# A graph layer on one core: three PSUM banks in turn for the row sums, and exponentials written to SBUF in place

## The chip, the core and the metric

The kernel runs on one core of a Trainium2 chip. The core has four compute engines that work side by side, each through its own list of instructions in order: TensorE (PE, matrix products into PSUM), VectorE (DVE), ScalarE (ACT) and GpSimd (POOL). SyncE (SP) issues DMA transfers. They meet through semaphores. PSUM has eight banks of 128 partitions by 512 f32. The metric is the device time of one execution in microseconds (us), lower is better. A difference of about 0.3% is what the measurement can tell from no change.

## What is computed

One layer of a graph network on 6250 nodes with 128 features and 100000 edges sorted by destination:

```python
a_k = exp(relu(concat(h[src], h[dst]) @ W_att_k + b_att_k))     # k = 1, 2, 3, one number per edge
att_k = segment_sum(a_k, dst)
avg_a = (a_1 / att_1[dst] + a_2 / att_2[dst] + a_3 / att_3[dst]) / 3
m = avg_a * relu(relu(relu(h[src] @ W1 + b1) @ W2 + b2) @ W3 + b3)
h_neigh = segment_sum(m, dst) / maximum(degree, 1)
out = relu(concat(h, h_neigh) @ Wc1 + bc1) @ Wc2 + bc2
return layernorm(x + out)
```

## The kernel before

The message of an edge depends on its source node alone, so the kernel first makes a table in HBM with a row of 128 message features and 3 logits for each node (up to about 56 us). Then it works through the edges in groups of 256 (two tiles of 128 edges). The first 94 groups, whose destinations are the 384 nodes with the most edges, are not gathered. For them VectorE and TensorE count how many edges run between each source and each of these nodes (the counting stage, one-hot products of L1428 added to `counts` by L1711). The dense stage then multiplies these counts by the exponentials of all 49 blocks of 128 source nodes against the 384 nodes.

The other 297 groups are cut into 126 units, `first_order`. Unit 0 has two groups, units 1 to 23 have four, the rest two (the last one). For each tile of a unit GpSimd issues one gather, an indirect DMA that fetches 128 rows of the table into a ring of 12 places (`gath`, L1226). In nine early units (3, 5, ... 19) the second pair of groups is not gathered, because its messages are computed directly, so the gathers are 558. Unit n has to be summed before its places in the ring are used again.

All engines walk the same loop over steps i = 0 ... 125. What matters in a step, in each engine's own order:

- TensorE: `add_edges(i)` (L1405 sums the weighted rows of unit i, L1411 the sums of the weights), counting products in the first 24 steps, `edge_q(i + 2)` (L1357, the query products: destination one-hots times the logits of the destinations, and in early units also L1361, the source logits), in the dense stage `hot_edges` (L1445), later pieces of the final layers (L883, L890, L894, L900).
- VectorE: in the dense stage `hot_weights(b, 0)` (L1741), then for unit i + 1 the logits (L1814, L1820; the latter is the first to need the gathered rows) and the weights (L1840, L1845), then `hot_weights(b, 1)`, `one_hot(i + 3)` (L1772), `hot_weights(b, 2)`, then `add_sums(i - 1)` (L1862), which adds the PSUM sums of a unit to `acc` in SBUF and sets `s_acc`, then final pieces.
- ScalarE: in the dense stage relu (L1509, `hot_logits`) and exp (L1518, `hot_exp`) of the 128 x 384 logits of a block and an attention head k, and for each unit the copy L1579 and the exp L1539.
- GpSimd: only the gathers, unit after unit, each preceded by a wait on `s_sum` for the unit that held the place.

The dense stage covers steps 26 to 76. Unit i sums into bank 0 or 2 in turn, so `add_edges(i)` waits until VectorE has added unit i - 2. The dense exponentials go to one PSUM bank (`EXP_BANK`, bank 4): `hot_exp` waits until the `hot_weights` before it has read the bank (`s_hw`). The final layers of the nodes that are complete start at about step 80 and end with the last units.

Of the kernel before, what the change touches and what calls it, by code (L numbers as in the profile page):

```python
# [32 lines left out]
P = 128  # L33
HEADS = 3
# [4 lines left out]
CHUNK = 4  # L39
# [17 lines left out]
TWO, THREE = 2, 3  # L57
# [35 lines left out]
def gnn_program(nc, x, x_t, src, dst, w_first, w_rest, b_rows, table, hot_table, near_table, q_table, early_table, out,  # L93
# [59 lines left out]
    with ctx:  # L153
# [910 lines left out]
        def edge_pass(first):  # L1064
# [53 lines left out]
            def q_bank(i):  # L1118

                return Q_BANKS[0] if i < n_long else Q_BANKS[i % TWO]  # L1120

            def q_user(i):

                return max((n for n in range(i) if q_bank(n) == q_bank(i)), default=-1)

            def from_q(i):

                n, c = n_tiles(i), PARTS + width(i)
                return bank[q_bank(i)][:, 0:n * c].rearrange("p (t c) -> p t c", t=n)
# [5 lines left out]
            def rows_of(i):  # L1135

                at = place[i] % RING * CHUNK
                return gath[:, at:at + n_tiles(i), :]
# [72 lines left out]
            with Straight(nc) if first else nc.Block() as block:  # L1211
# [118 lines left out]
                def _(pe):  # L1330
# [13 lines left out]
                    def edge_q(i):  # L1344

                        q_landed(pe, i)
                        one_hot_ready(pe, i)
                        if q_user(i) >= 0:
                            pe.wait_ge(s_wt, q_user(i) + 1)
                        elif first and q_bank(i) == EARLY_BANK:  # L1350
                            pe.wait_ge(s_erow, EARLY)
                        k = early(i)
                        if k is not None:
                            pe.wait_ge(s_ecopy, k + 1)
                        for t in range(n_tiles(i)):
                            mine = k is not None and t >= CHUNK
                            last = pe.matmul(from_q(i)[:, t, :], near_of(i)[:, t * P:(t + 1) * P],  # L1357
                                             q_eye[:, slot(i, t // TILES), 0:PARTS + width(i)],
                                             start=True, stop=not mine)
                            if mine:  # L1360
                                last = pe.matmul(from_q(i)[:, t, 0:HEADS],  # L1361
                                                 early_x[:, (t - CHUNK) * P:(t - CHUNK + 1) * P], w_logit[:, 0:HEADS],
                                                 start=False, stop=True)
                        last.then_inc(s_q, 1)

                    def turn_early(k):
# [25 lines left out]
                        last.then_inc(s_e3, 1)  # L1392

                    def add_edges(i):
                        sums, rows_here, w = bank[SUM_BANKS[i % TWO]], rows_of(i), width(i)
                        pe.wait_ge(s_wt, i + 1)
                        if early(i) is not None:
                            pe.wait_ge(s_emsg, early(i) + 1)
                        if i >= TWO:
                            pe.wait_ge(s_acc, groups_to(i - TWO))  # L1400
                        for j in range(len(order[i])):
                            at = j * (HEADS + 1) * w
                            for h in range(TILES):
                                t = j * TILES + h
                                pe.matmul(sums[:, at:at + HEADS * w], rows_here[:, t, 0:P], wt_of(i)[:, t, :],  # L1405
                                          start=h == 0, stop=h == TILES - 1)
                        for j in range(len(order[i])):
                            at = j * (HEADS + 1) * w
                            for h in range(TILES):
                                t = j * TILES + h  # L1410
                                last = pe.matmul(sums[SUMS_AT:SUMS_AT + HEADS + 1, at + HEADS * w:at + HEADS * w + w],  # L1411
                                                 a_col[:, i % THREE, t, :], mask_of(i)[:, t, :],
                                                 start=h == 0, stop=h == TILES - 1)
                        last.then_inc(s_sum, len(order[i]))
# [83 lines left out]
                def _(act):  # L1498
                    def hot_logits(b, k):

                        m = block_nodes(b)
                        if b == 0:
                            act.wait_ge(s_hl, 16 * (HEADS * HOT + 1))
                            act.wait_ge(s_cadd, n_hot)
                        act.wait_ge(s_hb[b % BLOCKS], 16 * (b // BLOCKS + 1))
                        n = HEADS * b + k
                        if n >= TWO:
                            act.wait_ge(s_he, n - TWO + 1)
                        act.activation(hot_logit[0:m, n % TWO, :], hot_ld[0:m, k, :], ACT.Relu,  # L1509
                                       bias=hot_block[0:m, b % BLOCKS, 1 + P + k:2 + P + k]).then_inc(s_hr, 1)  # L1510

                    def hot_exp(b, k):

                        m, n = block_nodes(b), HEADS * b + k
                        act.wait_ge(s_hr, n + 1)
                        if n >= 1:
                            act.wait_ge(s_hw, n)
                        act.activation(bank[EXP_BANK][0:m, 0:hot_nodes], hot_logit[0:m, n % TWO, :],  # L1518
                                       ACT.Exp).then_inc(s_he, 1)

                    def one_hot(i):

# [120 lines left out]
                def _(dve):  # L1643
# [92 lines left out]
                    def hot_weights(b, k):  # L1736
                        m, n = block_nodes(b), HEADS * b + k
                        dve.wait_ge(s_he, n + 1)
                        if b >= THREE:
                            dve.wait_ge(s_hm, b - THREE + 1)  # L1740
                        dve.scalar_tensor_tensor(hot_wt[0:m, b % THREE, k, :], bank[EXP_BANK][0:m, 0:hot_nodes],  # L1741
                                                 FLT_MAX, counts[0:m, b, :], ALU.min, ALU.mult).then_inc(s_hw, 1)

                    def copy_hot():
# [105 lines left out]
                    def add_sums(i):  # L1850
                        w = width(i)
                        if first and i == 0:
                            dve.wait_ge(s_zero, zeroed)
                        dve.wait_ge(s_sum, groups_to(i))
                        for j, g in enumerate(order[i]):
                            start = window(g)
                            done = groups_to(i) - len(order[i]) + j
                            if done >= 1:
                                dve.wait_ge(s_acc, done)
                            sums, at = bank[SUM_BANKS[i % TWO]], j * (HEADS + 1) * w  # L1860
                            here = acc[:, :, bass.ds(start, w)]
                            dve.tensor_tensor(here, here, sums[:, at:at + (HEADS + 1) * w].rearrange(  # L1862
                                "p (k w) -> p k w", w=w), ALU.add).then_inc(s_acc, 1)
# [154 lines left out]
```

## Time and profile before

| | |
|---|---|
| median of 3 runs | 783.3 us (783.0 to 785.25) |
| the profiled execution | 783.88 us, of which the span from the first to the last instruction is 779.9 us |
| busy share of the span | PE 80%, DVE 75%, POOL 73%, PE weight loads 66%, ACT 54% |
| mean granted TensorE clock | 0.876 of full speed |

A busy share is an average over the whole span. The profile also says what ended each idle time of an engine, in square brackets behind a row of the timeline or as totals. "issue" means that the engine waited for nothing that the profile shows. Line numbers (L1226) are those of the kernel before.

### The profile page before, as it was taken

Reading aid. Unit: us, or ns where it says so; the run is one execution under the profiler, and the core shown is the slowest. Engines: PE = TensorE matmul, PEld = TensorE weight load, DVE = VectorE, ACT = ScalarE, POOL = GpSimd, SP = SyncE. Lnnn points to the kernel's source line nnn. Section 1 sums busy time; section 2 is a strip of 40 time slices with the busy share of each in tenths; the row PEclk is TensorE's granted clock in tenths of the full one; section 3 lists DMA queues with packets and bytes.
Section 4 is the critical chain, followed back from the end, with each engine's and each line's share of the span. In section 5 each row is a group of like instructions: output and inputs, shape, how many; then the busy total and the mean of one; then the engine's idle time right before and its main releaser. Section 6 shows DMA issues by size and latency. Waiting matters only on the chain.

```text
span 779.9 us, 17410 instructions
## 1 busy us (share of the span) xinstructions
PE 623.2 (80%) x5133; PEld 510.9 (66%) x5133; DVE 585.6 (75%) x1946; ACT 420.3 (54%) x1048; POOL 571.7 (73%) x605
## 2 busy tenths in 40 slices
PE   8951989999977676989787878788887878678775
PEld 5741676667655445878787777777676766557664
DVE  4886576787889697777777777777887878887876
ACT  6565676767656343767676766674123322333323
POOL 7777777777777777777777777777777777777760
PEclk9985677878788775899999999999998989999897
DMA  8974333333872333333333333333534444454421
GB/s 228 253 188 95 78 82 78 83 78 81 66 92 63 67 91 84 76 82 77 81 79 79 81 78 82 77 83 70 137 94 118 109 104 108 104 134 104 100 56 35
DMA packets 82743, 75.15 MB, mean 96 GB/s; under 512 B 34873, under 2 KB 66401, under 8 KB 82641
## 3 DMA queue, kind: packets, MB, share of 16 engines
q0 software_dynamic: 19008, 39.82, 25.7%
q1 hardware_dynamic: 63344, 34.00, 15.9%
q8 instruction: 44, 0.72, 0.4%
q14 instruction: 59, 0.48, 0.2%
q10 hardware_dynamic: 288, 0.13, 0.1%
HBM read 64.62 MB, written 9.26 MB: 95 GB/s over the span
## 4 chain that ended last, share of the span: by engine, by line
DVE 38%; PE 26%; ACT 15%; issue 15%; DVEq 3%; DMA 2%; ACTq 0%; POOL 0%; SPq 0%
DVE fin L1741 10%; PE bank L1405 6%; ACT bank L1518 6%; DVE acc L1862 4%; PE bank L1428 4%; PE bank L883 3%; DVE fin L974 3%; DVE work L1840 3%; DVE side L1772 3%; DVE counts L1711 2%; ACT fin L1553 2%; DVE work L1845 2%; ACT work L1539 2%; PE bank L1411 2%; DVE fin L1698 2%
## 5 line engine op out<-in xcount | busy, mean ns | idle before, releaser
L1226 POOL DMA_INDIRECT work<-message_table,src_t x558 | 531.6, 953 | 170.1 <-issue 166.8
L1405 PE MATMUL bank<-work 128*128 128x144 f32 (+8 forms) x1188 | 187.6, 313 | 56.3 <-DVE acc L1862 56.0
L1405 PEld LDWEIGHTS bank<-work 128*128 128x128 f32 x1188 | 172.6, 221 | 71.1 <-issue 70.7
L1579 ACT COPY work<-bank 128x192 f32<-128x192 f32 (+7 forms) x126 | 37.3, 296 | 197.3 <-DVE work L1814 187.8
L1445 PE MATMUL bank<-work,fin 128*128 128x129 f32 (+1 forms) x882 | 114.5, 285 | 0.0
L1862 DVE TENSOR_TENSOR acc<-acc,bank 128x192 f32 (+8 forms) x297 | 88.7, 299 | 31.3 <-issue 6.9
L1518 ACT ACTIVATE bank<-hot_logit 128x384 f32<-128x384 f32 (+1 forms) x147 | 72.7, 494 | 69.9 <-DVE fin L1741 60.3
L1445 PEld LDWEIGHTS bank<-work,fin 128*128 128x128 f32 (+1 forms) x882 | 105.2, 196 | 2.2 <-issue 0.2
L1845 DVE TENSOR_TENSOR work<-bank,work 128x576 f32<-128x576 f32 (+7 forms) x126 | 86.2, 684 | 13.5 <-DVE work L1840 0.5
L1741 DVE SCALAR_TENSOR_TENSOR fin<-bank,counts 128x384 f32<-128x384 f32 (+1 forms) x147 | 81.4, 554 | 16.9 <-ACT bank L1518 16.4
L1509 ACT ACTIVATE hot_logit<-logits_or_x,work 128x384 f32<-128x384 f32 (+1 forms) x147 | 88.2, 600 | 0.0
L883 PE MATMUL bank<-rest_w,acc 128*128 128x128 f32 x294 | 46.7, 318 | 32.9 <-DVE fin L974 29.1
L1428 PE MATMUL bank<-fin 128*128 128x294 bf16 (+2 forms) x188 | 50.2, 408 | 21.1 <-ACT fin L1558 17.1
L883 PEld LDWEIGHTS bank<-rest_w,acc 128*128 128x128 f32 x294 | 41.6, 223 | 35.3 <-DVE fin L974 30.3
L1411 PE MATMUL bank<-work 128*4 128x48 f32 (+8 forms) x1188 | 64.2, 203 | 0.0
L1711 DVE TENSOR_TENSOR counts<-counts,bank 128x294 f32 (+2 forms) x94 | 56.3, 599 | 8.2 <-issue 7.3
L1553 ACT ACTIVATE fin<-fin 128x128 bf16<-128x128 f16 x188 | 59.3, 386 | 0.0
L1357 PE MATMUL bank<-side 48*128 48x57 bf16 (+8 forms) x594 | 41.4, 185 | 20.4 <-DVE side L1772 15.1
L1840 DVE TENSOR_SCALAR work<-work 128x12 f32<-128x12 f32 (+1 forms) x126 | 25.7, 204 | 42.0 <-ACT work L1539 38.9
L1698 DVE TENSOR_SCALAR fin<-fin 128x294 bf16<-128x294 f16 (+2 forms) x188 | 56.1, 342 | 0.0
L1411 PEld LDWEIGHTS bank<-work 128*4 128x4 f32 x1188 | 45.5, 89 | 15.7 <-issue 2.6
L1772 DVE TENSOR_SCALAR side<-side,less_col 48x512 bf16<-48x512 bf16 x149 | 54.2, 376 | 0.7 <-DMA side<-near_nodes 0.6
(153 smaller groups left out, 780.0 us busy)
## 6 DMA issues: line engine op xcount, KB each, us to landing
work<-message_table,src_t POOLq DMA_INDIRECT x558
side<-near_nodes SPq DMA_DIRECT2D x102, 48.0 KB
side<-logit_parts SPq DMA_DIRECT2D x297, 0.8 KB
message_table<-work SPq DMA_DIRECT2D x12, 262.0 KB, 4.3
work<-message_table SPq DMA_DIRECT2D x48, 65.5 KB
work<-in_x_t SPq DMA_DIRECT2D x12, 256.0 KB, 4.2
fin<-in_x SPq DMA_DIRECT2D x11, 256.0 KB, 3.1
logits_or_x<-in_x_t SPq DMA_DIRECT2D x11, 256.0 KB, 3.5
```

The costliest lines, as they stand in the source:

```text
L883: last = pe.matmul(to[:, k * P:(k + 1) * P], acc[:, k, nodes], wc1[:, 1, :], start=True, stop=True)
L1226: pool.indirect_dma_start(out=rows_of(n)[:, t, :], out_offset=None, in_=table[:, :], in_offset=bass.IndirectOffsetOnAxis(ap=src_t[:, h, g: ...
L1405: pe.matmul(sums[:, at:at + HEADS * w], rows_here[:, t, 0:P], wt_of(i)[:, t, :], start=h == 0, stop=h == TILES - 1)
L1411: last = pe.matmul(sums[SUMS_AT:SUMS_AT + HEADS + 1, at + HEADS * w:at + HEADS * w + w], a_col[:, i % THREE, t, :], mask_of(i)[:, t, :], s ...
L1428: pe.matmul(bank[COUNT_BANKS[g % FOUR]][:, 0:n], hot_lo[:, t % HOT_RING, :], hot_comb[:, t % HOT_RING, 0:n], start=h == 0, stop=h == TILES ...
L1445: last = pe.matmul(bank[SIDE_BANKS[h]][:, k * (P + 1):(k + 1) * (P + 1)], hot_wt[0:m, b % THREE, k, h * P:(h + 1) * P], rows_here, start=F ...
L1509: act.activation(hot_logit[0:m, n % TWO, :], hot_ld[0:m, k, :], ACT.Relu, bias=hot_block[0:m, b % BLOCKS, 1 + P + k:2 + P + k]).then_inc(s ...
L1518: act.activation(bank[EXP_BANK][0:m, 0:hot_nodes], hot_logit[0:m, n % TWO, :], ACT.Exp).then_inc(s_he, 1)
L1741: dve.scalar_tensor_tensor(hot_wt[0:m, b % THREE, k, :], bank[EXP_BANK][0:m, 0:hot_nodes], FLT_MAX, counts[0:m, b, :], ALU.min, ALU.mult). ...
L1772: dve.tensor_scalar(here, here, less_col[0:WIN, 0:1], 0.0, ALU.add, ALU.is_equal).then_inc(s_eq, 1)
L1845: dve.tensor_tensor(wt_of(i).rearrange("p t (k w) -> p t k w", w=w), from_q(i)[:, :, PARTS:PARTS + w].unsqueeze(2).to_broadcast([P, n, HEA ...
L1862: dve.tensor_tensor(here, here, sums[:, at:at + (HEADS + 1) * w].rearrange("p (k w) -> p k w", w=w), ALU.add).then_inc(s_acc, 1)
```

## The change

Three edits. (1) From the unit behind step 26 on, the row sums go to banks 0, 2 and 4 in turn, so `add_edges(i)` waits for the unit that used its bank last, from unit 30 on the third before it. (2) Bank 4 becomes free for that because the dense exponentials are written over the relu's result in SBUF (`hot_logit`, two places in turn). `hot_weights` then reads `hot_logit` and `counts`, both in SBUF. The wait on `s_hw` moves from the exp to the relu two before. (3) In the nine early units the query products of all tiles come first, then the source logits of the second pair's four tiles.

```diff
+            def sum_bank(i):
+                return SUM_BANKS[i % TWO] if not first or i <= HOT_AT else (SUM_BANKS + (EXP_BANK,))[i % THREE]
+            def sum_user(i):
+                return max((n for n in range(i) if sum_bank(n) == sum_bank(i)), default=-1)
...
                         for t in range(n_tiles(i)):
-                            mine = k is not None and t >= CHUNK
                             last = pe.matmul(from_q(i)[:, t, :], near_of(i)[:, t * P:(t + 1) * P],
                                              q_eye[:, slot(i, t // TILES), 0:PARTS + width(i)],
-                                             start=True, stop=not mine)
-                            if mine:
-                                last = pe.matmul(from_q(i)[:, t, 0:HEADS],
-                                                 early_x[:, (t - CHUNK) * P:(t - CHUNK + 1) * P], w_logit[:, 0:HEADS],
-                                                 start=False, stop=True)
+                                             start=t == 0 if k is not None else True, stop=k is None)
+                        if k is not None:
+                            for t in range(CHUNK):
+                                last = pe.matmul(from_q(i)[:, CHUNK + t, 0:HEADS], early_x[:, t * P:(t + 1) * P],
+                                                 w_logit[:, 0:HEADS], start=False, stop=t == CHUNK - 1)
...
                     def add_edges(i):
-                        sums, rows_here, w = bank[SUM_BANKS[i % TWO]], rows_of(i), width(i)
+                        sums, rows_here, w = bank[sum_bank(i)], rows_of(i), width(i)
...
-                        if i >= TWO:
-                            pe.wait_ge(s_acc, groups_to(i - TWO))
+                        if sum_user(i) >= 0:
+                            pe.wait_ge(s_acc, groups_to(sum_user(i)))
+                        elif sum_bank(i) == EXP_BANK:
+                            pe.wait_ge(s_cadd, n_hot)
...
                         if n >= TWO:
-                            act.wait_ge(s_he, n - TWO + 1)
+                            act.wait_ge(s_hw, n - TWO + 1)
                         act.activation(hot_logit[0:m, n % TWO, :], hot_ld[0:m, k, :], ACT.Relu,
...
                         act.wait_ge(s_hr, n + 1)
-                        if n >= 1:
-                            act.wait_ge(s_hw, n)
-                        act.activation(bank[EXP_BANK][0:m, 0:hot_nodes], hot_logit[0:m, n % TWO, :],
-                                       ACT.Exp).then_inc(s_he, 1)
+                        here = hot_logit[0:m, n % TWO, :]
+                        act.activation(here, here, ACT.Exp).then_inc(s_he, 1)
...
-                        dve.scalar_tensor_tensor(hot_wt[0:m, b % THREE, k, :], bank[EXP_BANK][0:m, 0:hot_nodes],
+                        dve.scalar_tensor_tensor(hot_wt[0:m, b % THREE, k, :], hot_logit[0:m, n % TWO, :],
                                                  FLT_MAX, counts[0:m, b, :], ALU.min, ALU.mult).then_inc(s_hw, 1)
```

VectorE keeps its order. In a step of the dense stage it reads, before the change, L1741 being `hot_weights`, L1772 the one-hot, L1862 `add_sums`:

```order
L1845 TENSOR_TENSOR work<-bank,work 128x384 [waits s_a,s_mcopy]
L1741 SCALAR_TENSOR_TENSOR fin<-bank,counts 128x384 [waits s_he]
L1772 TENSOR_SCALAR side<-side,less_col 48x512 [waits s_near1]
L1741 SCALAR_TENSOR_TENSOR fin<-bank,counts 128x384 [waits s_he]
L1862 ISA [waits s_acc,s_sum]
L1862 TENSOR_TENSOR acc<-acc,bank 128x4x32
```

and in the changed kernel (its lines are 7 higher: L1748 is `hot_weights`):

```order
L1852 TENSOR_TENSOR work<-bank,work 128x384 [waits s_a,s_mcopy]
L1748 SCALAR_TENSOR_TENSOR fin<-hot_logit,counts 128x384 [waits s_he]
L1779 TENSOR_SCALAR side<-side,less_col 48x512 [waits s_near1]
L1748 SCALAR_TENSOR_TENSOR fin<-hot_logit,counts 128x384 [waits s_he]
L1869 ISA [waits s_acc,s_sum]
L1869 TENSOR_TENSOR acc<-acc,bank 128x4x32
```

No instruction moved. What changed is the first source of `hot_weights`, from a PSUM bank to SBUF.

ScalarE in the same stage, before (L1509 relu, L1518 exp, L1579 and L1539 the copy and exp of a unit):

```order
L1509 ACTIVATE hot_logit<-logits_or_x,work 128x384 [waits s_he,s_hb1]
L1518 ACTIVATE bank<-hot_logit 128x384 [waits s_hw,s_hr]
L1579 COPY work<-bank 128x128 [waits s_sum,s_qs]
L1539 ACTIVATE work<-work 128x12 [waits s_a,s_lg]
L1509 ACTIVATE hot_logit<-logits_or_x,work 128x384 [waits s_he,s_hb1]
```

and now (L1518 relu, L1526 exp):

```order
L1518 ACTIVATE hot_logit<-logits_or_x,work 128x384 [waits s_hw,s_hb1]
L1526 ACTIVATE hot_logit<-hot_logit 128x384 [waits s_hr]
L1586 COPY work<-bank 128x128 [waits s_sum,s_qs]
L1546 ACTIVATE work<-work 128x12 [waits s_a,s_lg]
L1518 ACTIVATE hot_logit<-logits_or_x,work 128x384 [waits s_hw,s_hb1]
```

Again the order stands, and the wait on `s_hw` has moved to the relu.

TensorE in the first early unit, before (L1357 query product, L1361 source logits):

```order
L1357 MATMUL bank<-side 128x29 [waits s_wt,s_ecopy,s_eq,s_qw3]
L1357 MATMUL bank<-side 128x29 x4
L1361 MATMUL bank<-rest_w,work 128x3
L1357 MATMUL bank<-side 128x29
L1361 MATMUL bank<-rest_w,work 128x3
L1357 MATMUL bank<-side 128x29
L1361 MATMUL bank<-rest_w,work 128x3
L1357 MATMUL bank<-side 128x29
L1361 MATMUL bank<-rest_w,work 128x3
```

and now (L1364 and L1369):

```order
L1364 MATMUL bank<-side 128x29 [waits s_wt,s_ecopy,s_eq,s_qw3]
L1364 MATMUL bank<-side 128x29 x7
L1369 MATMUL bank<-rest_w,work 128x3 x4
```

The same twelve products, in another order behind the same waits.

## Rows read from the trace of the kernel before

**Rows 1.** Line view, L1226: the gathers; duration in ns, idle time before them

```profile
L1226 POOL DMA_INDIRECT work<-message_table,src_t x558: 940/944/2132, 56.1 to 756.6; - x186
...
  issue: 166.8, 547
  PE bank L1411: 2.7, 9
```

**Rows 2.** Waits: engine line waited for: us in total, times, longest us

```profile
ACT bank L1518 <- DVE fin L1741: 60.3, 82, 1.4
PE bank L1405 <- DVE acc L1862: 56.0, 51, 3.2
```

**Rows 3.** Timeline: start, duration, instruction: 160th gather, logits of units 25, 122, 123

```profile
257.21 0.94 POOL L1226 DMA_INDIRECT work<-message_table,src_t  x1 [0.30 <-issue]
...
295.08 0.17 DVE L1820 TENSOR_TENSOR work<-work 128x12 f32<-128x12 f32 x1
...
746.19 0.18 DVE L1820 TENSOR_TENSOR work<-work 128x12 f32<-128x12 f32 x1 [0.57 <-DMA work<-message_table,src_t]
...
751.66 0.20 DVE L1820 TENSOR_TENSOR work<-work 128x12 f32<-128x12 f32 x1 [2.27 <-DMA work<-message_table,src_t]
```

**Rows 4.** Timeline of VectorE in one step of the dense stage

```profile
405.45 0.18 DVE L1814 TENSOR_REDUCE work<-bank 128x12 f32<-128x36 f32 x1
...
406.47 0.17 DVE L1840 TENSOR_SCALAR work<-work 128x12 f32<-128x12 f32 x1 [0.56 <-ACT work L1539]
...
408.44 0.56 DVE L1741 SCALAR_TENSOR_TENSOR fin<-bank,counts 128x384 f32<-128x384 f32 x1 [0.37 <-ACT bank L1518]
...
410.10 0.18 DVE L1814 TENSOR_REDUCE work<-bank 128x12 f32<-128x36 f32 x1
```

**Rows 5.** Timeline: gathers and L981, which reads two SBUF tensors

```profile
621.32 0.68 DVE L981 TENSOR_TENSOR fin<-fin,row_b 128x512 f32<-128x512 f32 x1
...
621.54 1.28 POOL L1226 DMA_INDIRECT work<-message_table,src_t  x1 [0.30 <-issue]
...
640.62 0.94 POOL L1226 DMA_INDIRECT work<-message_table,src_t  x1 [0.30 <-issue]
...
641.13 0.68 DVE L981 TENSOR_TENSOR fin<-fin,row_b 128x512 f32<-128x512 f32 x1
...
748.60 0.69 DVE L981 TENSOR_TENSOR fin<-fin,row_b 128x512 f32<-128x512 f32 x1
...
748.66 1.45 POOL L1226 DMA_INDIRECT work<-message_table,src_t  x1 [0.30 <-issue]
```

**Rows 6.** Timeline: first and last of 58 gathers begun within 0.43 us of an L1741

```profile
304.79 0.55 DVE L1741 SCALAR_TENSOR_TENSOR fin<-bank,counts 128x384 f32<-128x384 f32 x1
...
304.93 0.94 POOL L1226 DMA_INDIRECT work<-message_table,src_t  x1 [0.30 <-issue]
...
533.61 0.56 DVE L1741 SCALAR_TENSOR_TENSOR fin<-bank,counts 128x384 f32<-128x384 f32 x1 [0.37 <-ACT bank L1518]
...
534.01 0.94 POOL L1226 DMA_INDIRECT work<-message_table,src_t  x1 [0.30 <-issue]
```

**Rows 7.** Timeline and line view, early units: L1361, end of unit 14's sums, 20's first gather

```profile
L1361 PE MATMUL bank<-rest_w,work x72: 252/272/376, 91.7 to 240.0; 128*128 128x3 f32 x72
...
206.45 0.80 PE L1411 MATMUL bank<-work 128*4 128x24 f32 x16
...
208.02 0.96 POOL L1226 DMA_INDIRECT work<-message_table,src_t  x1 [0.30 <-issue]
```

**Rows 8.** Timeline of the last two units: last gather, weights and sums of unit 124

```profile
756.65 0.94 POOL L1226 DMA_INDIRECT work<-message_table,src_t  x1 [0.30 <-DMA work<-message_table,src_t]
...
757.69 0.76 DVE L1845 TENSOR_TENSOR work<-bank,work 128x576 f32<-128x576 f32 x1
...
759.93 2.23 PE L1405 MATMUL bank<-work 128*128 128x144 f32 x8 [2.51 <-DVE acc L1862]
...
762.00 0.17 DVE L1820 TENSOR_TENSOR work<-work 128x6 f32<-128x6 f32 x1
```

More of the change, by code:

```diff
@@ L1859, in add_sums @@
                                 dve.wait_ge(s_acc, done)
-                            sums, at = bank[SUM_BANKS[i % TWO]], j * (HEADS + 1) * w
+                            sums, at = bank[sum_bank(i)], j * (HEADS + 1) * w
                             here = acc[:, :, bass.ds(start, w)]
```

## The prediction

> **What bounds the kernel now.** I read the busy shares first. They don't decide: four engines lie between 54% and 80%. The list of waits tempts next. Its large entries are ScalarE's exp behind VectorE's `hot_weights` (60.3 us) and TensorE's `add_edges` behind `add_sums` (56.0 us) [rows 2], and these are what the edits shorten. But a wait is worth time only if the waiting engine sets the end, so I looked for an engine that never waits. The view of one line for the gathers shows it [rows 1]. GpSimd issues 558 of them from 56.1 to 756.6 us, one takes 944 ns (median), and before 547 of them it was idle for 0.30 us "behind nothing", the pause between two gathers. Nine more such pauses of 0.3 us are put down to TensorE and are no longer than the others. (756.6 - 56.1) / 557 is 1.258 us for each, and 0.944 + 0.305 is 1.249. So GpSimd ran without one stop from the end of the table to 23 us before the span's end.
>
> The other engines run behind it. I numbered the gathers by unit. Unit 25 is complete with the 160th gather, which ends at 258.15 us, and its rows are first read (L1820) at 295.08, 36.9 us later, the largest distance. At units 122 and 123 VectorE waits for the rows themselves (0.57 and 2.27 us) [rows 3]. A compute step of the dense stage takes 4.65 us in the one shown (405.45 to 410.10) [rows 4], four gathers 5.0 us, so the distance melts slowly. It has just gone when the gathers end. **GpSimd and the compute chain finish together, and only GpSimd can't be sped up by this change.** Whatever makes the compute faster lets it wait for rows sooner. Whatever lengthens the gathers moves the end one to one.
>
> **The change part by part.** *Third bank.* In the dense step shown `add_edges` would no longer wait for `add_sums`. Saved on TensorE, not on GpSimd: 0 at the end, except in the last units. There weights of unit 124 are ready at 757.69 + 0.76 = 758.45 and the products begin at 759.93 [rows 8], so the bank costs about 1.4 us. VectorE, however, is busy with final pieces until it turns to the last unit at 762.00, and its own order decides the rest. I take -0.3 us; the bounds are 0 and -2.9 (the last unit is read 4.4 us after its last gather ended at 757.59, where the best units need 1.5 [rows 3, 8]).
>
> *Exponentials in place.* The exp no longer waits for `hot_weights`. VectorE's wait of 0.37 us in a step goes, and part of the 0.56 us before L1840, because ScalarE gets to the unit's copy and exp sooner [rows 4]. That makes a step about 4.1 us. With gathers of 5.2 us a unit (below), the distance (by the same count some 33 us at the stage's start) is gone after about 33 / 1.1 = 30 of the 49 steps. Worth nothing at the end, for the same reason. The exp with an SBUF target may take up to the relu's time, which ScalarE has room for.
>
> *The new source of `hot_weights`.* This is the term that counts. L1741 reads `counts` in SBUF and the bank; now both tensors come from SBUF. The trace has such an operation, L981, 11 times, and it holds up gathers. One begun at 748.66, 0.06 us into an L981, took 1.45 us; one 0.22 us into another took 1.28; one begun 0.5 us ahead of an L981 took 0.94 [rows 5]. Taking the usual 0.94 from the long ones, both gathers went on 0.12 us before the L981's end (748.66 + 1.45 - 0.94 = 749.17 against 749.29; 621.88 against 622.00). So a gather whose start falls into such an operation stands until 0.12 us before its end; one already begun is not touched. All six L981 hits together: 1.52 us by this rule, 1.45 in the trace. L1741 with its PSUM source does nothing of the kind: 58 gathers began within 0.43 us (0.555 - 0.12) of the start of one of the 147 L1741, the first 0.14 and the last 0.40 us into it, and all took 0.94 or 0.95 [rows 6].
>
> The Trainium skill, page "SBUF — State Buffer", section "Who interferes with whom", says that a VectorE instruction with two SBUF inputs contends with a GpSimd instruction that reads SBUF, not with one that only writes, and infers that descriptor generation isn't touched. By that inference these gathers would keep their length and the sum would be 783.6 us. The L981 rows disagree with it, and I go by them.
>
> *Its price.* Put each of those 58 gathers off to 0.43 us after the L1741's start: the sum of (0.43 - offset) is 12.4 us. Chance alone gives the same: 0.43² / 2 / 1.25 = 0.074 us for each of 147 operations, 10.9 us. Two corrections. In the last 19 or so dense steps compute waits for rows, so its operations keep a fixed distance to the gathers. L1820 then starts 2.5 us after the start of the unit's last gather; the `hot_weights` behind the weights starts 1.3 us later, at 3.8, and the gathers at 3.75 and 5.0 just miss it and its successor. The hits there may be none: 30/49 of 12.4 is 7.6. But the miss is by 0.05 us, and in the later finals the same lock puts an L981 right on a gather's start (as at 748.60), about +1 us. I take 10 + 1 = 11 us, between 7.6 and 13.4.
>
> *Query products first.* L1361 takes 272 ns [rows 7] and stays 8 records a unit; four fewer changes between the two kinds of product may save 0.2 us in each early unit on TensorE, in a stage in which GpSimd doesn't wait: 0. It would cost only if it were slower, from a point I can name: unit 20's first gather needs the place of unit 14, whose sums ended at 207.25, and began at 208.02 [rows 7], 0.77 us of slack, the smallest anywhere. Six early units lie ahead of it; 0.3 us more in each would cost 1 us.
>
> Sum against the profiled execution: 783.88 + 11 - 0.3 = 794.6. It lies 0.6 above the median of the runs, so 794.0.
>
> **The rivals.** *The operations block as one (slower still).* VectorE's order is `hot_weights`, one-hot, `hot_weights`. Now that the exps are ready ahead, the three stand end to end for about 1.3 us. If GpSimd can't get in between them, a gather waits up to 0.73 + 0.43 = 1.16 us, and a step costs (0.43² + 1.16²) / 2.5 = 0.61 us instead of 0.22: 18 us over the first 30 steps, up to 30 over all. Time 802 to 813. Against it: at 621.54 the gather got in although the next VectorE operation followed at once [rows 5], but that one reads PSUM. Chance 0.17.
>
> *No hold-up at all.* The scalar form with a 16-bit second source may not behave as L981 does. GpSimd then ends at 757.6 as before and the time is 783.3 - 0.3 = 783.0, the same. Chance 0.12.
>
> *Faster.* The same, and the tail takes all it can: 783.3 - 2.9 = 780.4. It needs no hold-up and the last unit read 1.5 us after its gather, though VectorE's pieces ahead of it are untouched. A reader of the waits alone would promise more, 49 x (4.65 - 4.1) = 27 us in the dense stage. It fails on the gathers' 1.25 us beat. It decides if GpSimd's pauses turn out to be waits for the other engines; 547 equal pauses of 0.30 speak against it. Chance 0.06.
>
> **How the numbers follow.** Main case 0.65: 794, own range 788 to 799. With the blocking rival at 0.17 the slower side has 0.82; within 0.3% (2.4 us, about what a measurement of this kernel can tell from no change) 0.12; faster 0.06. The range leaves out the two cases without hold-up (0.18 in all) and takes in the lower half of the blocking one: 787 to 808.
>
> **What the profile will show.** The line view of the gathers: median still 0.944, mean up from 0.953 by about 0.02, with durations up to 1.37 only where `hot_weights` started shortly before; the last gather at about 767 instead of 756.6. ScalarE's wait behind `hot_weights` and TensorE's behind `add_sums` nearly gone in the dense stage. VectorE waiting for rows (4 times before) in most units from about unit 60 on. If the last gather still starts near 757, the hold-up is wrong; if gathers of over 1.4 us are common in the dense stage, they block as one; if the hits are few although operations and gathers overlap at random, the rule of the 0.12 us is wrong; if the gathers show waits for TensorE, the ring was the limit.

## The result and the profile after

The changed kernel takes 795.5 us (median of 4 runs, 793.7 to 796.2) against 783.15: ratio 1.0146, 95% interval 1.0124 to 1.0169 (a ratio here is not the quotient of the two medians, which would be 1.0157). Forecast were 794, a range of 787 to 808, and slower. The profiled execution took 794.8 us with a span of 791.0.

The page of the changed kernel, its chain that ended last (section 4) and the gathers' line of section 5 (busy us, mean ns, idle before):

```profile
POOL 38%; PE 22%; issue 16%; DVE 11%; ACT 5%; DMA 4%; SPq 1%; DVEq 1%; another core or an unknown queue 1%; POOLq 0%; ACTq 0%
...
L1234 POOL DMA_INDIRECT work<-message_table,src_t x558 | 544.4, 976 | 170.8 <-issue 168.6
```

GpSimd's gathers are now the largest share of the chain; before, the same list gave them 0% and DVE 38%. The line view of the gathers, which answers to [rows 1]:

```profile
L1234 POOL DMA_INDIRECT work<-message_table,src_t x558: 940/944/1753, 55.2 to 768.5; - x186
...
  issue: 168.6, 553
```

Still 558 gathers, still a median of 944 ns and pauses of 0.30 us. The mean went from 953 to 976 ns. The excess (what the gathers took above 0.944 us each), summed over all gathers, was 4.9 us before and is 17.7 now, and of that the stretch from 300 to 545 us holds 0.5 before and 13.2 now. The first gather started 0.9 us earlier, so the last one starts 12.8 - 0.9 = 11.9 us later (756.6 to 768.5), and the span is 11.1 us longer. The rest, 0.7 us with rounding, is the tail, from the last gather's start to the end: 23.2 us before, 22.5 now.

The waits that the edits aimed at are shorter, and a new one has come (us in total, times, longest):

```profile
DVE work L1827 <- DMA work<-message_table,src_t: 62.7, 44, 4.4
...
ACT hot_logit L1518 <- DVE fin L1748: 22.1, 48, 1.0
...
PE bank L1414 <- DVE acc L1869: 15.1, 8, 4.3
```

ScalarE's wait behind `hot_weights` fell from 60.3 to 22.1 us and TensorE's behind `add_sums` from 56.0 to 15.1 [rows 2]. VectorE waits 62.7 us for rows. Compute has caught up with the gathers at unit 53 (rows read 1.8 us after the last gather ended), where before it still lagged by 26.6 us, and there it waits.

One step of the dense stage in the timeline of the changed kernel. L1748 is `hot_weights`, L1779 the one-hot:

```profile
341.02 0.55 DVE L1748 SCALAR_TENSOR_TENSOR fin<-hot_logit,counts 128x384 f32<-128x384 f32 x1
341.49 0.34 DVE L1779 TENSOR_SCALAR side<-side,less_col 48x512 bf16<-48x512 bf16 x1
341.75 0.54 DVE L1748 SCALAR_TENSOR_TENSOR fin<-hot_logit,counts 128x384 f32<-128x384 f32 x1
342.22 0.70 DVE L1869 TENSOR_TENSOR acc<-acc,bank 128x128 f32 x2
342.87 0.56 DVE L1748 SCALAR_TENSOR_TENSOR fin<-hot_logit,counts 128x384 f32<-128x384 f32 x1
```

and its gathers:

```profile
340.73 0.95 POOL L1234 DMA_INDIRECT work<-message_table,src_t  x1 [0.30 <-PE bank L1420]
341.98 1.13 POOL L1234 DMA_INDIRECT work<-message_table,src_t  x1 [0.30 <-issue]
343.42 0.94 POOL L1234 DMA_INDIRECT work<-message_table,src_t  x1 [0.30 <-issue]
344.67 0.95 POOL L1234 DMA_INDIRECT work<-message_table,src_t  x1 [0.30 <-issue]
345.92 1.12 POOL L1234 DMA_INDIRECT work<-message_table,src_t  x1 [0.30 <-issue]
```

The gather of 341.98 falls 0.23 us into the second L1748 and took 1.13 us. 341.98 + 1.13 - 0.94 = 342.17, and the operation ended at 342.29: 0.12 before its end, as in [rows 5]. The next one starts 0.55 us into the third L1748, just late enough. And 3.94 us on (345.92) the picture repeats. Three gathers (3.74 us) and one hold-up (0.18) make one VectorE step (3.92). The two engines have locked: between 300 and 405 us, 29 gathers are long, about one in each step.

Once compute waits for rows, they lock in another way, again with about one hit in each unit (24 between 405 and 535 us). Gathers of the changed kernel:

```profile
465.33 0.94 POOL L1234 DMA_INDIRECT work<-message_table,src_t  x1 [0.30 <-issue]
466.58 1.22 POOL L1234 DMA_INDIRECT work<-message_table,src_t  x1 [0.30 <-issue]
468.10 0.94 POOL L1234 DMA_INDIRECT work<-message_table,src_t  x1 [0.30 <-issue]
469.35 0.94 POOL L1234 DMA_INDIRECT work<-message_table,src_t  x1 [0.30 <-issue]
470.60 0.94 POOL L1234 DMA_INDIRECT work<-message_table,src_t  x1 [0.30 <-issue]
471.84 1.22 POOL L1234 DMA_INDIRECT work<-message_table,src_t  x1 [0.30 <-issue]
```

The unit takes 5.26 us (466.58 to 471.84), 0.28 more than four undisturbed gathers.

Eight of the 53 long gathers between 300 and 535 us were held over more than one VectorE instruction (1.37 to 1.57 us). They make 4.0 of the 13.2 us.

### The profile page after: what moved, and what is told of

Its sections match the earlier page's. It is cut to its first block, busy times and chain, and to the rows that moved or that the text cites. A ratio compares the mean times of both kernels' runs of the same rounds, so it can differ in the third digit from the quotient of the medians.

```text
span 791.0 us, 17264 instructions
## 1 busy us (share of the span) xinstructions
PE 622.0 (79%) x5133; PEld 510.6 (65%) x5133; DVE 579.7 (73%) x1946; ACT 429.4 (54%) x1048; POOL 584.7 (74%) x605
## 3 DMA queue, kind: packets, MB, share of 16 engines
q1 hardware_dynamic: 63344, 34.00, 15.9%
## 4 chain that ended last, share of the span: by engine, by line
POOL 38%; PE 22%; issue 16%; DVE 11%; ACT 5%; DMA 4%; SPq 1%; DVEq 1%; another core or an unknown queue 1%; POOLq 0%; ACTq 0%
POOL work L1234 38%; PE bank L1414 5%; PE bank L1437 3%; DVE counts L1718 2%; PE bank L1454 2%; DVE acc L1869 2%; DVE fin L1705 2%; ACT fin L1560 1%; PE bank L1420 1%; PE bank L601 1%; PE bank L580 1%; PE bank L589 1%; ACT counts L1615 1%; ACT fin L1565 1%
## 5 line engine op out<-in xcount | busy, mean ns | idle before, releaser
L1234 POOL DMA_INDIRECT work<-message_table,src_t x558 | 544.4, 976 | 170.8 <-issue 168.6
L1454 PE MATMUL bank<-work,fin 128*128 128x129 f32 (+1 forms) x882 | 117.1, 290 | 0.0
L1454 PEld LDWEIGHTS bank<-work,fin 128*128 128x128 f32 (+1 forms) x882 | 108.0, 200 | 2.5 <-issue 0.6
L1518 ACT ACTIVATE hot_logit<-logits_or_x,work 128x384 f32<-128x384 f32 (+1 forms) x147 | 89.0, 605 | 22.2 <-DVE fin L1748 22.1
L883 PE MATMUL bank<-rest_w,acc 128*128 128x128 f32 x294 | 51.3, 340 | 44.6 <-DVE fin L974 34.3
L1748 DVE SCALAR_TENSOR_TENSOR fin<-hot_logit,counts 128x384 f32<-128x384 f32 (+1 forms) x147 | 80.6, 549 | 2.0 <-PE bank L1454 2.0
L1526 ACT ACTIVATE hot_logit<-hot_logit 128x384 f32<-128x384 f32 (+1 forms) x147 | 76.9, 523 | 4.7
L883 PEld LDWEIGHTS bank<-rest_w,acc 128*128 128x128 f32 x294 | 45.6, 242 | 46.9 <-DVE fin L974 35.6
L1827 DVE TENSOR_TENSOR work<-work 128x12 f32<-128x12 f32 (+1 forms) x126 | 22.0, 175 | 72.0 <-DMA work<-message_table,src_t 62.7
L1420 PEld LDWEIGHTS bank<-work 128*4 128x4 f32 x1188 | 45.8, 89 | 15.9 <-issue 3.3
L1364 PE MATMUL bank<-side 48*128 48x57 bf16 (+8 forms) x594 | 37.0, 184 | 24.1 <-DMA side<-logit_parts 17.8
L1546 ACT ACTIVATE work<-work 128x12 f32<-128x12 f32 (+1 forms) x126 | 27.0, 214 | 50.4 <-DVE work L1827 47.7
```

The costliest lines, as they stand in the source:

```text
L883: last = pe.matmul(to[:, k * P:(k + 1) * P], acc[:, k, nodes], wc1[:, 1, :], start=True, stop=True)
L1234: pool.indirect_dma_start(out=rows_of(n)[:, t, :], out_offset=None, in_=table[:, :], in_offset=bass.IndirectOffsetOnAxis(ap=src_t[:, h, g: ...
L1454: last = pe.matmul(bank[SIDE_BANKS[h]][:, k * (P + 1):(k + 1) * (P + 1)], hot_wt[0:m, b % THREE, k, h * P:(h + 1) * P], rows_here, start=F ...
L1526: act.activation(here, here, ACT.Exp).then_inc(s_he, 1)
L1748: dve.scalar_tensor_tensor(hot_wt[0:m, b % THREE, k, :], hot_logit[0:m, n % TWO, :], FLT_MAX, counts[0:m, b, :], ALU.min, ALU.mult).then_i ...
```

## The experiments

Theory: the second SBUF source of `hot_weights` holds up the gathers, and these set the end. Rivals: the banks or the moved waits cost the time; the early units; compute, not GpSimd, is the bound.

### The source alone

The kernel before with one operand changed. It reads the relu's result, so the exp is left out of the dense stage.

```diff
-dve.scalar_tensor_tensor(hot_wt[0:m, b % THREE, k, :], bank[EXP_BANK][0:m, 0:hot_nodes],
+dve.scalar_tensor_tensor(hot_wt[0:m, b % THREE, k, :], hot_logit[0:m, n % TWO, :],
```

> The kernel before with one operand changed: hot_weights reads the relu's result in SBUF, not the exponentials in the PSUM bank. Its waits, banks and order stay as they were, so the dense counts are weighted with numbers that lack the exp. Theory (a gather that begins while VectorE reads two SBUF tensors stands until 0.12 us before the operation's end, and the gathers set the end): with VectorE's step still about 4.7 us the overlaps are those counted in the trace of before, so the dense gathers get about 12 us longer, the last one starts near 768 us, and the time is 793 to 797. Rival (the relaxed waits or the third bank make the changed kernel slow, not the source): 783, gathers as before.

Measured: 787.6 us, ratio 1.0042 (1.0020 to 1.0063). Slower as the theory says, but by a third of the amount: the expected 793 to 797 was missed. Between 300 and 535 us the hold-ups sum to 4.5 us, not 12. Two things are seen in its trace. The hits are few: 14 long gathers begun in a `hot_weights`, where 58 had begun in one before. And there is the reverse case (VectorE, then GpSimd, of this run):

```profile
412.20 0.55 DVE L1741 SCALAR_TENSOR_TENSOR fin<-hot_logit,counts 128x384 f32<-128x384 f32 x1
412.67 0.54 DVE L1772 TENSOR_SCALAR side<-side,less_col 48x512 bf16<-48x512 bf16 x1
413.37 0.62 DVE L1741 SCALAR_TENSOR_TENSOR fin<-hot_logit,counts 128x384 f32<-128x384 f32 x1 [0.16 <-ACT bank L1518]
```

```profile
412.15 0.95 POOL L1226 DMA_INDIRECT work<-message_table,src_t  x1 [0.30 <-issue]
413.41 0.94 POOL L1226 DMA_INDIRECT work<-message_table,src_t  x1 [0.30 <-issue]
```

The gather of 413.41 begins 0.04 us into an L1741 and isn't held up; instead the L1741 takes 0.62 us. With the old waits the three `hot_weights` of a step stand 1.17 to 1.25 us apart, nearly the gathers' own beat. So in the kernel before, where nothing is held up, the offsets come in runs: gathers begin 0.13, 0.21 and 0.28 us into the L1741 of 312.28, 313.45 and 314.63. A first held-up gather of such a run would move those behind it out of the windows. That explains the few hits; it is read from the offsets, not tested by itself. My count had held up each of the 58 by itself.

### The changed kernel with two banks

```diff
-return SUM_BANKS[i % TWO] if not first or i <= HOT_AT else (SUM_BANKS + (EXP_BANK,))[i % THREE]
+return SUM_BANKS[i % TWO]
```

> The changed kernel without its third bank: sums in two banks in turn, exponentials in place, query products first. Theory: the two SBUF sources are still there, gathers 9 to 14 us longer in the dense stage, time 792 to 798, like the changed kernel; the bank is worth at most 1 us in the tail. Rival (the third bank, in which TensorE sums while VectorE adds, causes the loss): 783.

Measured: 795.5 us, ratio 1.0149 (1.0110 to 1.0187), the hold-ups 17.3 us in all. The loss is the same without the bank. Only one gather between 300 and 535 us is held over more than one instruction here, against eight in the changed kernel, so such long hits don't explain the loss either.

### The same, but `hot_weights` reads PSUM

Two banks, the waits of the changed kernel, and the operand back in bank 4, which nothing writes any more (so stale numbers stand for the exponentials).

```diff
-dve.scalar_tensor_tensor(hot_wt[0:m, b % THREE, k, :], hot_logit[0:m, n % TWO, :],
+dve.scalar_tensor_tensor(hot_wt[0:m, b % THREE, k, :], bank[EXP_BANK][0:m, 0:hot_nodes],
```

> The same as the run with two banks, but hot_weights reads PSUM bank 4, which nothing writes in the dense stage any more (so the dense counts are weighted with stale numbers). The waits are those of the changed kernel. Theory: one SBUF source, no gather is held up, dense gathers 0.944 us, time 782 to 784, although compute steps are as short as in the changed kernel and wait for rows. Rival (the drift of the gathers' starts, or compute locked to the gathers, costs by itself): 787 or more.

Measured: 783.05 us, ratio 0.9994 (0.9974 to 1.0015). Its line view of the gathers:

```profile
L1234 POOL DMA_INDIRECT work<-message_table,src_t x558: 940/944/2019, 56.7 to 756.4; - x186
```

The last gather starts at 756.4, and between 300 and 535 us the excess is 0.3 us, nearly all of it from four gathers begun in a one-hot, although 63 gathers began within 0.43 us of a `hot_weights`. One of them, 0.28 us into it:

```profile
343.06 0.55 DVE L1748 SCALAR_TENSOR_TENSOR fin<-bank,counts 128x384 f32<-128x384 f32 x1
343.34 0.94 POOL L1234 DMA_INDIRECT work<-message_table,src_t  x1 [0.30 <-issue]
```

One operand is the difference to the run above, and it is worth 12.5 us. This settles that the loss comes from the source of `hot_weights`.

### The query products alone

The kernel before with the third edit only (the diff of the change above).

> The kernel before with the third edit alone, the query products of an early unit first. Theory: TensorE saves some tenths of a us in each early unit, GpSimd does not wait there, so the time is 783, within 0.3%; the slack of the ring at unit 20 grows from 0.8 us. Rival: the later source logits delay VectorE and the ring blocks GpSimd: 785 or more.

Measured: 783.5 us, ratio 0.9998 (0.9979 to 1.0017). No effect on the time. In its profile the compute chain is far ahead of the kernel before's (unit 26 is read 23.9 us after its gathers, against 36.4; slack of the ring at unit 20: 12.3 us against 0.8). VectorE waits for rows in 19 units, where it did in 4, and the end doesn't move: faster compute alone is worth nothing.

### The changed kernel with the old exp wait

```diff
                         act.wait_ge(s_hr, n + 1)
+                        if n >= 1:
+                            act.wait_ge(s_hw, n)
                         here = hot_logit[0:m, n % TWO, :]
```

> The changed kernel (three banks, exponentials in place, two SBUF sources) with one wait put back: the exp waits again for the hot_weights before it. VectorE's step in the dense stage is then long again (4.5 us or more in place of 3.9). Theory: the hold-up needs the source and the short step, in which three gathers and one hold-up fit; with the old step the gathers are pushed out of the windows after one hit, as in the run that changed the source alone (4 us of hold-up): 786 to 790. Rival (two SBUF sources cost the same at any step, and the run with the source alone was spared by its phases): 793 to 797.

Measured: 788.5 us, ratio 1.0066 (1.0048 to 1.0085). Three banks, in place, two SBUF sources, and yet 7 us less than the changed kernel; hold-ups of 3.9 us between 300 and 535. VectorE's step there is 4.8 us (units 26 to 53 in 129.8 us), against 4.2 in the changed kernel. So the size of the loss depends on both: with the SBUF source, the two runs with the old waits have 4.5 and 3.9 us of hold-ups in the stage, the two with the new ones 13.2 and 12.5. The wait changes two things at once, the length of the step and the spacing inside it (the three `hot_weights` stand 1.20 and 1.21 us apart, in the changed kernel 0.73 and 1.12), and which of them decides was not separated. Compute waits for rows in only two units of this run, both before the dense stage, so gathers alone don't set its end; its last gather starts 3.3 us later than in the kernel before and 8.6 earlier than in the changed one.

### `hot_weights` in three pieces

```diff
-dve.scalar_tensor_tensor(hot_wt[0:m, b % THREE, k, :], hot_logit[0:m, n % TWO, :], ...
+for a in range(0, hot_nodes, P):
+    last = dve.scalar_tensor_tensor(hot_wt[0:m, b % THREE, k, a:a + P], hot_logit[0:m, n % TWO, a:a + P], ...
```

> The changed kernel with each hot_weights cut into three operations of 128 columns (128 + about 150 cycles of overhead each, some 0.29 us, the three take 0.3 us more than the one). If a held-up gather goes on 0.12 us before the end of the operation it fell into, none in the dense stage stands longer than 0.17 us for a hot_weights, so its duration stays under 1.15 us, and the time falls to 787 to 791. If GpSimd cannot get in between operations that stand end to end, durations reach 1.4 us and more as in the changed kernel or longer, and the time is 795 to 802.

Measured: 806.3 us, ratio 1.0288 (1.0269 to 1.0307), the second branch, and 4 us above its 795 to 802. The hold-ups are 8 us more than in the changed kernel. The rest is not theirs: in the profile the first gather starts 1.8 us later and the tail is 2.1 us longer. VectorE and the gather of this run:

```profile
342.99 0.34 DVE L1782 TENSOR_SCALAR side<-side,less_col 48x512 bf16<-48x512 bf16 x1
343.25 0.68 DVE L1749 SCALAR_TENSOR_TENSOR fin<-hot_logit,counts 128x128 f32<-128x128 f32 x3
343.86 0.70 DVE L1872 TENSOR_TENSOR acc<-acc,bank 128x128 f32 x2
```

```profile
343.37 1.39 POOL L1234 DMA_INDIRECT work<-message_table,src_t  x1 [0.31 <-issue]
```

343.37 + 1.39 - 0.94 = 343.82 is 0.11 us before the end of the third piece. The gather had begun in the first. GpSimd does not get in between such operations; here it waits for the end of the whole row of them. The changed kernel has the same case, one-hot and second `hot_weights` end to end:

```profile
317.71 0.34 DVE L1779 TENSOR_SCALAR side<-side,less_col 48x512 bf16<-48x512 bf16 x1
317.97 0.55 DVE L1748 SCALAR_TENSOR_TENSOR fin<-hot_logit,counts 128x384 f32<-128x384 f32 x1
```

```profile
317.91 1.43 POOL L1234 DMA_INDIRECT work<-message_table,src_t  x1 [0.30 <-issue]
```

It began in L1779 and went on at 318.40, 0.12 us before the L1748's end. In the run with the PSUM source the row is cut there: its gather of 335.79 began 0.15 us into an L1779 with an L1748 close behind, and took only 1.00 us.

### The third bank behind the dense stage

Query products first, exponentials in their PSUM bank, three banks only from unit 78 on:

```diff
+return SUM_BANKS[i % TWO] if not first or i <= hot_end else (SUM_BANKS + (EXP_BANK,))[i % THREE]
```

> The kernel before with query products first and the third bank only behind the dense stage (from unit 78 on), the dense exponentials staying in their PSUM bank. Theory: no gather is held up that was not before; the bank is worth what it gave the changed kernel behind its last gather, 0.7 us: 782.4, not told from 783 (0.997 to 1.001). Rival (three banks in turn let compute wait for less and are worth what the waits on add_sums promise, behind the dense stage some 15 us): under 775.

Measured: 784.8 us, ratio 1.0010 (0.9998 to 1.0023). No gain from the bank that could be told, and the rival's 15 us are excluded.

### Less work for GpSimd

The kernel above with ten early units (one more in `STORE_AT`, the ones column of `hot_block` set two steps later) and a smaller memset:

```diff
-EARLY = 9
+EARLY = 10
-ACT_WORDS, POOL_FIRST, POOL_LAST = 1000, 2000, 3200
+ACT_WORDS, POOL_FIRST, POOL_LAST = 1000, 2000, 100
```

> The late-bank kernel with ten early units in place of nine (four gathers move from behind the table to ahead of it) and with 3100 of the 3200 columns that GpSimd sets to zero ahead of its first table gather given to ScalarE (2.78 us on GpSimd before). Theory (GpSimd's own work from the start to the last gather is the kernel's length): the early gather costs GpSimd what the later one saves, and the memset goes: 782.4 - 2.7 = 779.7, ratio 0.995 to 0.997. Rival (the engines behind the gathers set the length): the ratio is 1.000, or over it since TensorE and ScalarE get more to do.

Measured: 783.1 us, ratio 0.9995 (0.9978 to 1.0012). Its profile shows the last gather at 753.3, 3.3 us earlier than before, and a span of 777.7, but the median of 12 runs (779.5 to 786.5) doesn't carry it. The expected 0.995 to 0.997 lies outside the interval, and the rival's 1.000 inside it. Less work for GpSimd was worth nothing that can be told here, as it would be if compute is the next bound right behind it; but TensorE and ScalarE also got more to do in this run, and the two were not separated.

### Twelve gathers left out, before and after

The last tile of every fourth unit of the dense stage isn't gathered, its wait counts one less; its 128 edges get stale rows.

```diff
+def short(i):
+    return int(first and HOT_AT < i <= HOT_AT + 48 and i % 4 == 3)
...
+if t == CHUNK - 1 and short(n):
+    continue
```

> The kernel before with twelve gathers left out (the last tile of every fourth unit of the dense stage, whose 128 edges then get stale rows), 15.0 us less for GpSimd. If GpSimd and the compute chain finish together in the kernel before, compute becomes the bound at once and the time falls by little: 778 to 783. If GpSimd alone is the bound with the others well behind it in need, it falls by the whole 15: 768.

> The changed kernel with the same twelve gathers left out. Its compute waits for rows from unit 53 on, so it can follow: by the gathers' view the time falls by the 15.0 us, to 780 to 782. If the loss of the changed kernel were on the compute side, the time would stay at 790 or more.

Measured for this first pair: 982 and 984 us. On that chip the kernel before itself took 1014 us, and in the profiles of the pair GpSimd waited 132 and 116 us for releasers outside the core, so they tell nothing of the question. The same two kernels on another chip:

> Once more, since the first pair ran on a chip on which the kernel before took 1014 us. The kernel before with twelve gathers left out (the last tile of every fourth unit of the dense stage, whose 128 edges then get stale rows), 15.0 us less for GpSimd. If GpSimd and the compute chain finish together in the kernel before, compute becomes the bound at once and the time falls by little: 778 to 783. If GpSimd alone is the bound, with compute well able to follow, it falls by the whole 15: 768.

> Once more, for the same reason. The changed kernel with the same twelve gathers left out. Its compute waits for rows from unit 53 on, so it can follow: the time falls by the 15.0 us, to 780 to 782. If the loss of the changed kernel were on the compute side, the time would stay at 790 or more.

Measured: before with twelve less 780.5 us, ratio 0.9957 (0.9916 to 0.9998); changed with twelve less 781.9, ratio to the kernel before 0.9950 (0.9920 to 0.9980), 13.6 us below the changed kernel's 795.5 of another session, or some 15 us by the two ratios (1.0146 and 0.9950). In the first the last gather starts at 740.8 us, 15.9 earlier, but the span is only 6 us shorter. GpSimd's and VectorE's part of the trace (line views):

```profile
L1232 POOL DMA_INDIRECT work<-message_table,src_t x546: 940/944/1417, 56.4 to 740.8; - x182
...
  DVE work L1826: 5.7, 2
```

```profile
L1240 POOL DMA_INDIRECT work<-message_table,src_t x546: 940/944/2217, 55.8 to 754.7; - x182
...
  DVE work L1833: 52.9, 36
```

The last row of each is who waited for the gathers. In the kernel before with twelve less VectorE waits twice: compute has become the bound. In the changed one it still waits 36 times.

## Why the prediction was right

**What bounds the kernel: right.** GpSimd never stops in any profile of the kernel before or after. Taking twelve gathers out, 15.0 us of its work, gives back 13.6 to 15 us in the changed kernel. In the kernel before, where both chains ended together, it gives 4.7 by the medians, and by the interval anything from 0.2 to 6.6.

**The source of `hot_weights`: right, and shown.** The runs with and without the SBUF source, all else equal, are 795.5 and 783.05. The 0.12 us rule read from six L981 held for the new operation to 0.01 us.

The Trainium skill, page "SBUF — State Buffer", section "Who interferes with whom", says that a VectorE instruction with two SBUF inputs contends with a GpSimd instruction that reads SBUF. The traces agree if a gather counts as such a one: it takes its row numbers from `src_t`, which lies in SBUF. The prediction read the page's inference on descriptor generation as saying that the gathers keep their length, and they didn't. Whether the reading of the row numbers or the making of the descriptors is what waits, no run separates, so the inference itself stays open.

**The price: right in sum, wrong in how it was made up.** Forecast were 10 us for the dense stage and 1 for later pieces; measured 12.7 more in the stage and nothing behind it (1.2 us of excess from 535 us on, 1.6 before). Part of the hit is luck: three steps behind the 10 were off, and their errors partly cancel. (a) "Put each of those 58 gathers off" counts hits as independent; with the old step they are not, and the source alone cost 3 to 4 us. (b) "The hits there may be none" for the steps in which compute waits: 6.6 us there (405 to 535), as much as in the drifting steps ahead of it (6.6 from 300 to 405). (c) I took the operations as separate; rows of them block as one. (a) made the sum too large, (b) too small, and (c) too small by part of the 4.0 us of the eight gathers held over a row, though the run with two banks lost as much with one of them. As far as the traces show, the price is set by the beat on which the two engines lock: about one hit a VectorE step of 3.92 us (0.18 in the one shown), then one a unit of 5.26 (0.28).

**The moved waits: half right.** Worth nothing at the end, as said: alone with a PSUM source 783.05. But they weren't neutral. With them the hits settle into each step: 7 us of the 12 go when one wait is put back.

**The third bank: right that it is worth next to nothing; the 0.3 us is not shown.** `add_edges` of the last unit starts 6.7 to 6.8 us after the start of the last gather in the changed kernel, with the late bank and with three pieces, and 7.4 to 7.5 in the kernel before and the runs with two banks. But the tail doesn't follow it: 22.3 to 24.2 us in five profiles with two banks, 22.5 to 24.6 in those with three. The 0.7 us between the kernel before and the changed one lie within that spread.

**Query products first: right for the time; its worth in the stage is open.** I said 0.2 us a unit, which no run shows. In the profiles with this edit the compute lag at unit 26 is 22.7 to 37.8 us, against 36.4 and 37.7 in the kernel before and the run with the source alone. It goes roughly with the mean TensorE clock granted from 100 to 200 us, as a share of full speed: 0.78 before and 36.4 us, 0.80 and 37.8 in the PSUM-source run, 0.85 and 30.1 in the changed kernel, 0.91 and 23.9 in the query-first run. Whether the edit helps the clock or the executions differ by themselves was not separated and stays open; nothing of it reached the end.

**The rivals.** "The operations block as one" is true of the mechanism and not of the size: eight gathers in the dense stage fell into a row of them, not one in each step. "No hold-up" and "faster" are out.

**What the profile was to show.** The last gather (768.5 for about 767), the mean (up 0.023 for 0.02) and VectorE's waits for rows (from unit 52 for about 60) came out nearly as said. ScalarE's wait behind `hot_weights` did not go: 22.1 us of it stand before the relu, to which the wait on `s_hw` moved. And gathers took up to 1.57 us in the stage, not up to 1.37.

## What to carry to other kernels

Look for the engine that never waits before looking at the longest waits: two waits of 60 and 56 us were cut by two thirds and the kernel got slower. When a VectorE operand moves from PSUM to SBUF beside another SBUF operand, count the GpSimd-issued DMAs that run beside it, and don't split such operations into pieces that stand end to end. Where two periodic engines disturb each other, don't multiply a mean hold-up by a count; ask on which beat they lock, since one moved wait (7 us here) changes it.

## What the runs showed of the hardware

- A gather that begins while VectorE runs an instruction with two SBUF sources goes on 0.11 to 0.13 us before the end of that instruction, or of the whole row of such instructions standing end to end (1.39 us in place of 0.94 with three pieces of 0.28 us). Begun earlier than it, the gather is not touched, nor was one begun 0.04 us into it (413.41 in the run with the source alone).
- The other way is small: that `hot_weights` took 0.62 in place of 0.55 us.
- With one source in PSUM, none of 58 and of 63 gathers in the same position was held up.
- One-hots of 0.34 us with a single SBUF tensor (L1772) hold gathers up too, in the kernel before: 1.07 us for one begun 0.09 us into it (317.42), with nothing close behind it. With an operation of 1.21 us on two SBUF tensors (L1781) right behind the one-hot, a gather took 2.13 us (77.50).
